# Order of a projection piece and a score product in the quarters of two attention layers

## The reference

```python
x = x + attention(layernorm(x))                        # causal, 16 heads of 32
x = x + cross_attention(layernorm(x), ctx, pad_mask)   # 512 keys, 16 heads of 32
x = x + experts(layernorm(x))                          # 8 experts, the best one for each row
```

## Time and profile before

| | us |
|---|---|
| median of 3 runs (1942.8 to 1944.03) | 1942.85 |
| the profiled execution, its time | 1944.94 |
| its span in the profile | 1943.4 |
| TensorE busy | 1857.1 (96%) |
| VectorE busy | 1330.3 (68%) |
| ScalarE busy | 1121.6 (58%) |
| GpSimd busy | 951.7 (49%) |

### The profile page before, as it was taken

The page is one execution under the profiler, slowest core; times in us unless marked ns, Lnnn a source line. Parts: engine busy times, 40 slices in busy tenths (PEclk is TensorE's granted clock), DMA queues, the critical chain, the costliest instruction groups (busy, mean ns, idle before and its releaser), DMA issues. The chain is left out here.

```text
span 1943.4 us, 34689 instructions
## 1 busy us (share of the span) xinstructions
PE 1857.1 (96%) x10902; PEld 1311.6 (67%) x10902; DVE 1330.3 (68%) x2838; ACT 1121.6 (58%) x2156; POOL 951.7 (49%) x1136
## 2 busy tenths in 40 slices
PE   6999999999999989999999999999999985899997
PEld 4667777777777766666666666666666544799996
DVE  5667667676767676767575766666676556688886
ACT  3555555555555565656565655555565453788885
POOL 3445545554555455544455554545554343454442
PEclk9999999999999999999999999999999997899999
DMA  5554554546455564445455354534443644843221
GB/s 171 140 142 110 133 126 112 136 112 145 99 120 124 133 179 122 109 123 131 109 120 116 84 128 93 140 89 113 105 106 81 174 131 133 319 140 90 82 82 28
DMA packets 135159, 239.60 MB, mean 123 GB/s; under 512 B 29962, under 2 KB 31282, under 8 KB 134928
## 3 DMA queue, kind: packets, MB, share of 16 engines
q1 hardware_dynamic: 105920, 184.47, 34.8%
q0 software_dynamic: 22192, 51.66, 13.1%
q10 hardware_dynamic: 6880, 1.40, 0.4%
HBM read 112.99 MB, written 47.40 MB: 83 GB/s over the span
## 5 line engine op out<-in xcount | busy, mean ns | idle before, releaser
L621 ACT ACTIVATE attn_probs<-attn_sT 128x512 f32<-128x512 f32 (+3 forms) x1024 | 528.9, 518 | 467.4 <-PE attn_sT L976 464.4
L525 POOL TENSOR_TENSOR attn_probs<-attn_probs 128x512 f32<-128x512 f32 (+2 forms) x384 | 530.8, 1403 | 172.3 <-PE attn_o_ps L991 122.2
L750 DVE TENSOR_REDUCE attn_m_col<-attn_sS 128x1 f32<-128x512 f32 x512 | 342.6, 687 | 204.8 <-PE attn_sS L960 197.1
L976 PE MATMUL attn_sT<-attn_stack 98*128 98x512 f32 (+2 forms) x1024 | 386.2, 388 | 0.0
L960 PE MATMUL attn_sS<-attn_stack 97*128 97x512 f32 (+2 forms) x1024 | 368.0, 369 | 11.2 <-issue 2.6
L756 DVE CUSTOM_DVE_ANT_0 attn_sS<-attn_sS,attn_cT_low 128x128 f32<-128x128 f32 x496 | 240.9, 504 | 172.6 <-PE attn_sS L960 169.0
L976 PEld LDWEIGHTS attn_sT<-attn_stack 98*128 98x128 f32 x1024 | 187.7, 188 | 203.5 <-ACT attn_probs L621 128.7
L513 POOL TENSOR_SCALAR_AFFINE_SELECT attn_probs<-attn_probs 128x256 f32<-128x256 f32 x256 | 119.5, 467 | 347.2 <-ACT attn_probs L621 347.2
L991 PE MATMUL attn_o_ps<-attn_probs,attn_V 128*32 128x512 f32 (+3 forms) x2048 | 231.8, 523 | 5.1 <-ACT attn_probs L621 2.0
L960 PEld LDWEIGHTS attn_sS<-attn_stack 97*128 97x128 f32 x1024 | 193.8, 190 | 63.4 <-DVE attn_m_col L750 9.6
L940 PE MATMUL attn_pj<-attn_xT_high,attn_w_high 128*128 128x512 f32 x384 | 154.3, 402 | 1.4 <-DVE attn_xT_low L734 1.4
(11 more groups left out here) (237 smaller groups left out, 3639.3 us busy)
## 6 DMA issues: line engine op xcount, KB each, us to landing
attn_stack<-attn_stage SPq DMA_DIRECT2D x666, 128.0 KB, 2.3
attn_rows<-in_x_dram SPq DMA_DIRECT2D x64, 256.0 KB, 4.2
attn_rows<-x_after_self SPq DMA_DIRECT2D x64, 256.0 KB, 4.3
experts<-in_L_ffn_W_dram SPq DMA_DIRECT2D x16, 1024.0 KB, 14.4
attn_stack<-attn_stage POOLq DMA_DIRECT2D x96, 128.0 KB, 3.3
x_after_self<-attn_rows SPq DMA_DIRECT2D x32, 256.0 KB, 2.6
x_after_self<-in_L_attn_b_dense_dram POOLq DMA_DIRECT2D x32, 256.0 KB, 4.9
attn_rows<-in_ctx_dram SPq DMA_DIRECT2D x32, 256.0 KB, 3.0
```

The lines of the kernel that those rows point to most:

```text
L525: pool.tensor_tensor(total, total, tile_of(n, kb)[:, js, q0:S], ALU.add).then_inc(added, 1)
L621: act.activation(tile_of(n, kb)[:, j, q0:S], sT[:, i % 2, q0:S], ACT.Exp, scale=SCALE).then_inc(exp_done, 1)
L750: dve.tensor_reduce(to, sS[:, k % 2], AX_X, ALU.max).then_inc(s_free, 1)
L976: pe.matmul(sT[:, i % 2, q0:S], stack[0:ROW_MAX + 1, n % 2, 1, j, kb * P:(kb + 1) * P], stack[0:ROW_MAX + 1, n % 2, 0, j, q0:S], start=Tru ...
```

## The change

In a quarter that has a piece of a projection, the first plain score product is issued behind the first piece and no longer in front of it. In quarters without a piece nothing changes. Only TensorE's order is touched; no instruction is added or removed, and no wait is changed. The programs of the other engines stay as they are.

```diff
                 if in_groups(n) and q:
                     scores_T(n, q // J, q % J)
-                for key in found[:1]:
-                    scores(key)
+                if not parts:
+                    for key in found[:1]:
+                        scores(key)
                 if q == Q - 1 and turned_s(n, q):
                     turn(turned_s(n, q))
...
                 for u, k in parts[:1]:
                     chunk(u, k)
+                if parts:
+                    for key in found[:1]:
+                        scores(key)
```

## The result

| | before | after |
|---|---|---|
| median of 4 runs each, us | 1942.82 | 1993.28 |
| lowest to highest | 1941.76 to 1944.03 | 1990.2 to 1994.18 |
| profiled execution, its span | 1944.94, 1943.4 | 1993.41, 1991.8 |

The ratio is 1.0255, 95% interval 1.0242 to 1.0268: slower by about 50 us, inside the forecast's range (1970 to 2000) and 10 us over the forecast.

A forecast was written before the change was run, and what follows sets the result against it. The prediction took TensorE, busy for 96% of the span, to bound the kernel. Self groups 20.7 us less 1.5, cross groups 19.2 and heads 2 summed to 40.4 us more, so 1983 us was forecast, range 1970 to 2000.

The forecast's parts named there:

- TensorE has nothing to give, so each new wait counts in full: Whole kernel: TensorE is busy for 96% of the span, so each microsecond it stands still is one of the kernel.
- Quarters 1 and 2 cost TensorE nothing: Quarter 2's maximum, after 1.17 us of idle VectorE, starts 0.70 later at no TensorE cost; `divide` behind it starts later too.
- Quarters 3 and 4, 0.57 and 0.63: Main term: the load of (1,2) waits for (1,0)'s bank, costing 0.57 us per self group and 0.63 per cross group.
- The formula for a late load, L - w + 0.10: A weight load late by L, normally running ahead by w (0.23 for 512 columns), costs TensorE L - w + 0.10 us.
- A late load costs 0.10: TensorE: a late weight load is exposed for 0.10 us; were loads always hidden, the sum would be some 7 us less.
- Quarters 5 to 8: Self groups lose 0.12 us; cross groups save 0.15 at (2,2) in quarter 7, lose 0.12 in quarter 8, net -0.03.
- Heads, 2 us: Queries' `low_of_qk` ends 0.70 later, delaying SyncE's head DMAs; group 20 keeps 0.17 of 0.87 us slack; 2 us in all.
- R3: Rival, a larger loss: head 0 late in most groups, 40 us plus 60 x 0.4 = 24, so 2007; chance 0.08.
- The rest, zero: Earlier unit ends, ScalarE's exponentials and DMAs for rows of later quarters were priced at zero.
- The signs: Expected: maxima's idle time before line 960 18 to over 40 us; (1,2) 0.6 later; VectorE idles longer in quarters 1, 2.
- R1: Rival, not slower: a piece in front gives a product's bank 0.70 us more; 1918 to 1943, middle 1930; chance 0.02.
- R2: Rival, a small loss: quarter 4's wait replaces one PV has anyway, 0.2 us in 62 groups, so 1955; chance 0.06.

The follow-up runs named there:

- the first: Order before the change, with the score product moved behind the piece in quarter 2 alone: 1980.07 us, ratio 1.0188 to the kernel before.
- the fourth experiment: Order before with quarter 2's product alone moved, and on VectorE `divide` put in front of quarter 2's maximum: 1946.48 us, ratio 1.0018 to the kernel before.

## Why the prediction was right, and where its size was off

- *TensorE has nothing to give, so each new wait counts in full.* Right: the quarters' sums, 49.3 us, make up the difference. Two waits cost more than themselves, since the granted clock fell behind them: 4.2 us that the prediction had not counted.
- *Quarters 1 and 2 cost TensorE nothing.* Right: quarter 2 has the same length, to 0.3 us over all groups of a layer; quarter 1 is longer in group 1 alone, by 0.9 us at the lower clock. The delay that `divide` hands on is what mattered, and the first and the fourth experiment show it.
- *Quarters 3 and 4, 0.57 and 0.63.* Measured 16.1 / 30 = 0.54 and 19.7 / 32 = 0.62. The formula for a late load, L - w + 0.10, held: 0.78 of idle loads' time less the 0.04 that always stands there is 0.74, less 0.23, plus 0.10 is 0.61. The remark that the term hardly hangs on VectorE's queue was right for the change as a whole, and only as a pair: either cause gives 34 to 37 us alone, so that to remove one leaves the other's.
- *A late load costs 0.10.* The product at 1111.10 is followed by PV after 0.43; one on time is followed after 0.33 (1073.91 to 1074.24). So the weighing against the Trainium skill's rule (TensorE: Matmul & The Clock Gate, "Step-by-step: what each phase is for") came out as the row had it: loads run ahead of matmuls, as the rule says, but not past their own wait.
- *Quarters 5 to 8.* The signs and sizes of all four were right (table above).
- *Heads, 2 us.* This is the step that was mis-sized. That `low_of_qk` of the queries ends 0.70 later was right (it ends 0.86 us after the start of quarter 12 in group 20 before, 1.56 after), and that a group like 20 keeps some slack too. Wrong was to take a group where SyncE issues at its usual pace as the rule, and to price the others at 2 in all. In the groups where an issue takes 1.5 us, or a mask row or another load comes in between, nothing was left: 9.2 us by the trace, and by the experiments' medians, each against the kernel before on its own chip, 8.7 (without quarter 11), 11.5 (quarter 11 alone) and 13.5 (`low_of_qk` ahead, which also takes waits away that were there before). The high bound held 10 for it. R3 was this mechanism at 24 us; it came less than half way.
- *The rest, zero.* Not quite: the transposes of quarter 15 wait in seven cross groups, 2.7 us. The prediction went through what VectorE has queued behind the maxima, but not the row statistics behind quarter 9's.
- *The signs.* One half failed: VectorE idles longer before the maximum of quarter 1 (3.24 and not 2.55 us in group 44), but not before that of quarter 2 (1.18 and 1.17), since the product ahead of it was moved as well.
- *R1 and R2.* No trace of them: (1,2) waits in full, and the gain in quarter 7 is 4.4 us. R1's idea, that a product behind a piece gives VectorE time, is true of that one place.

What stays open: why the executions of the kernel without quarter 11 spread over 8 us, and whether the others have late heads too; why VectorE's operations are so long beside GpSimd's additions; and which moved quarter brings the transposes' wait. The traces point to quarter 9; the wait stays without quarters 2 and 3 and without quarter 11, and is not there with 2, 3, 7 or 11 moved alone.

## What to carry to other kernels

Before moving an instruction that another engine consumes, look at what is queued behind its consumer: the idle time in front of the consumer hides its own delay, but not that of the operation which waits in line behind it and was ready all along. With two buffers, count the distance between the two uses of the same one, not the distance to the next use; here a release takes 1.18 us and the new distance was 0.70. A slack of 0.87 us read in one group is not the slack of all groups: read its minimum, above all where a DMA queue stands in between.

## What was not expected of the hardware

The issue of a DMA on SyncE took 1.48 us where its neighbours took 0.59 and 0.71. The same issue took 1.18 us before the change and was covered; with 0.70 us less in front of the load it became a wait of about 1 us. VectorE operations that take 0.75 or 0.92 us elsewhere took 2.23 to 2.64 us beside GpSimd's additions. Three of the waits of 1 to 3 us on TensorE were followed by 3 to 7 us at a granted clock of 0.50; a wait of 1.91 us in the kernel before was not. Two sufficient causes of one wait measured 37 and 34 us alone and 40 together.
